# Shorter last chunks, weighted two fours per round, in the attention layers of a graph network kernel

## The reference

```
xj = gl[src]                                       # gathered by edge
e = leaky_relu(xj + gr[dst] + edge_e, 0.2)
alpha = einsum('ehc,hc->eh', e, att_w)             # 4 heads of 32 channels
m = segment_max(alpha, dst); alpha = exp(alpha - m[dst])
denom = segment_sum(alpha, dst); alpha = alpha / (denom[dst] + 1e-16)
out = segment_sum(xj * alpha[..., None], dst) + bias
```

## Time and profile before

| | us |
|---|---|
| median of 3 runs | 8513.38 |
| lowest, highest | 8485.4, 8525.23 |
| the profiled execution, its own time | 8425.69 |
| its span | 8423.3 |
| attention layers, first copy of the first to L2080 of the last | 4345.1 to 8380.8 |

### The profile page before, as it was taken

The page is one execution under the profiler, slowest core; times in us unless marked ns, Lnnn a source line. Parts: engine busy times, 40 slices in busy tenths (PEclk is TensorE's granted clock), DMA queues, the critical chain, the costliest instruction groups (busy, mean ns, idle before and its releaser), DMA issues.

```text
span 8423.3 us, 124315 instructions
## 1 busy us (share of the span) xinstructions
PE 5549.1 (66%) x35700; PEld 4942.3 (59%) x35700; DVE 3931.2 (47%) x13695; ACT 3368.8 (40%) x12586; POOL 4633.3 (55%) x4868
## 2 busy tenths in 40 slices
PE   7445555577777667777746766765666675767676
PEld 5333333566667566677646666664666664666665
DVE  4222222366666566665644444452444443444445
ACT  2222221366666456666623333332333332333333
POOL 2555554366666356666426666626666653666562
PEclk9999999899998888888868888887888886888887
DMA  2110010344444234444313333323333332333332
GB/s 56 22 25 24 23 24 19 100 106 103 106 104 106 65 104 121 124 120 118 94 52 108 107 108 109 108 79 93 108 107 108 107 106 67 109 107 107 106 108 64
DMA packets 489685, 743.91 MB, mean 88 GB/s; under 512 B 219285, under 2 KB 351865, under 8 KB 487973
## 3 DMA queue, kind: packets, MB, share of 16 engines
q1 hardware_dynamic: 307764, 423.98, 16.2%
q0 software_dynamic: 180928, 305.59, 15.1%
q10 hardware_dynamic: 320, 6.40, 0.3%
HBM read 636.97 MB, written 97.83 MB: 87 GB/s over the span
## 4 chain that ended last, share of the span: by engine, by line
PE 18%; issue 13%; another core or an unknown queue 13%; DVE 12%; ACT 5%; DVEq 3%; POOL 0%; ACTq 0%; DMA 0%
DVE AR L1956 5%; PE PS L1368 4%; PE PS L1382 3%; PE PS L1259 2%; PE PS L1283 2%; PE PS L1280 2%; PE PS L1380 2%; DVEq L505 1%; ACT AR L1040 1%; DVE AR L1877 1%; PE PS L1393 1%; DVEq L1956 1%; ACT AR L936 1%; ACT AR L1029 1%
## 5 line engine op out<-in xcount | busy, mean ns | idle before, releaser
L577 POOL DMA_INDIRECT AR<-gtab_d,AR x2436 | 2308.9, 948 | 1523.0 <-issue 625.1
L569 POOL DMA_INDIRECT AR<-ptab_d,AR x1624 | 1545.9, 952 | 1006.0 <-issue 397.3
L1040 ACT ACTIVATE AR<-PS,AR 128x512 f32<-128x512 f32 x609 | 418.5, 687 | 2511.7 <-PE PS L1382 1218.6
L1368 PE MATMUL PS<-AR 128*112 128x132 f32 x4872 | 927.9, 331 | 688.9 <-DVE AR L1956 665.3
L1956 DVE TENSOR_TENSOR AR<-AR,PS 112x132 f32 x2436 | 696.0, 286 | 1191.8 <-issue 448.9
L1368 PEld LDWEIGHTS PS<-AR 128*112 128x112 f32 x4872 | 727.5, 209 | 827.0 <-DVE AR L1956 420.4
L551 POOL DMA_INDIRECT rec_d<-AR x782 | 753.0, 963 | 654.8 <-DVE AR L1563 431.0
L1382 PE MATMUL PS<-AR 128*128 128x128 f32 x4872 | 1024.7, 312 | 27.3 <-issue 27.1
L2033 DVE SCALAR_TENSOR_TENSOR AR<-PS,AR 128x512 f32<-128x512 f32 x609 | 455.2, 747 | 998.3 <-issue 567.8
L1382 PEld LDWEIGHTS PS<-AR 128*128 128x128 f32 x4872 | 898.7, 230 | 29.1 <-issue 28.7
L1259 PE MATMUL PS<-AR 128*112 128x161 f32 x3248 | 673.4, 335 | 340.5 <-DVE AR L1877 175.9
(11 more groups left out here) (345 smaller groups left out, 8872.9 us busy)
## 6 DMA issues: line engine op xcount, KB each, us to landing
AR<-ste_d SPq DMA_DIRECT2D x404, 512.0 KB
AR<-nbb_d SPq DMA_DIRECT2D x303, 224.0 KB
ste_d<-AR SPq DMA_DIRECT2D x101, 512.0 KB
AR<-gtab_d,AR POOLq DMA_INDIRECT x2436
AR<-ptab_d,AR POOLq DMA_INDIRECT x1624
nbb_d<-AR SPq DMA_DIRECT2D x101, 224.0 KB
AR<-key_d SPq DMA_DIRECT2D x94, 224.0 KB
AR<-rec_d SPq DMA_DIRECT2D x812, 8.0 KB
```

The costliest lines, as they stand in the source:

```text
L569: e.indirect_dma_start(out=XJ1[:, t % 32, :], out_offset=None, in_=tabs_d[0][:, :], in_offset=off).then_inc(done_, 16)
L577: e.indirect_dma_start(out=xj2(t)[:, t % 4, :], out_offset=None, in_=tabs_d[1][:, :], in_offset=off).then_inc(done_, 16)
L1368: x = e.matmul(PS[6 + v_ % 2][0:B, (t % 2) * 132:(t % 2 + 1) * 132], SQ4[:, i % 4, t % 4, :], PX[:, i % 5, t % 4, :, :].rearrange("p c h - ...
```

## The change

The ends of the chunks were 8, 16, ..., 184, 190, 195, 199, 203. They are now 8, 16, ..., 176, 182, 187, 192, 196, 200, 203: the last six chunks have 6, 5, 5, 4, 4 and 3 fours instead of the last five having 8, 6, 5, 4 and 4. There are 28 chunks instead of 27. Fours of chunks that end after 176 are weighted two per round, so that a chunk's fours are no longer spaced one per round behind its `back`. DVE gets the second weight of a round behind `leaked` and one add; ACT spreads the second four of a round behind the copy. `LASTR` falls from 217 to 211.

```diff
 def rounds_of_attention():
-    ends = list(range(8, 185, 8)) + [190, 195, 199, NQ]
+    ends = list(range(8, 177, 8)) + [182, 187, 192, 196, 200, NQ]
...
         back = max(turn + 3, px[-1] + 1 if px else 0)
         steps.append((turn, turn + 1, turn + 2, turn + 2, back))
-        px += [back + i for i in range(end - start)]
+        per = 1 if end <= 176 else 2
+        px += [back + i // per for i in range(end - start)]
...
+            def spread_out(l, i):
+                w.wait_ge(*nl_sem(l, i))
+                if i >= 4:
+                    w.wait_ge(s_scat2, pair_at(l, 2 * (i - 4) + 1))
+                done(e.activation(SQ4[:, i % 4, :, :], NBB[:, nb_slot(l, i), :, :], ACT.Copy), s_oh2)
...
-                    for i in weighted_in(j):
-                        w.wait_ge(*nl_sem(l, i))
...
+                    spread = weighted_in(j)
+                    for i in spread[:1]:
+                        spread_out(l, i)
                     if 0 <= j < NQ:
...
                         done(e.activation(LE[:, j % 2, :], PS[j % 2][:, :], ACT.Identity, bias=BRS[:, l % 2:l % 2 + 1], scale=0.2), s_le)
+                    for i in spread[1:]:
+                        spread_out(l, i)
...
                     if j < NQ:
                         leaked(j)
+                    if len(quads) > 1:
+                        add()
+                        weight(quads[1])
                     while tiles:
                         add()
```

More of the change, by code:

```diff
@@ L31, in rounds_of_attention @@
 def rounds_of_attention():
-    ends = list(range(8, 185, 8)) + [190, 195, 199, NQ]
+    ends = list(range(8, 177, 8)) + [182, 187, 192, 196, 200, NQ]
     px, steps, start = [], [], 0
-    for c, end in enumerate(ends):
+    for end in ends:
         turn = end + 1
@@ L1030, in scalar_program @@
                         done(x, s_ex)
-                    for i in weighted_in(j):
-                        w.wait_ge(*nl_sem(l, i))
-                        if i >= 4:
-                            w.wait_ge(s_scat2, pair_at(l, 2 * (i - 4) + 1))
-                        done(e.activation(SQ4[:, i % 4, :, :], NBB[:, nb_slot(l, i), :, :], ACT.Copy), s_oh2)
+                    spread = weighted_in(j)
+                    for i in spread[:1]:
+                        spread_out(l, i)
                     if 0 <= j < NQ:
```

## The result

The changed kernel has a median of 8531.27 us (22 runs, 8509.59 to 8750.88); the kernel before, run beside it, 8508.38 us (22 runs). The ratio is 1.0024, 95% interval 1.0016 to 1.0032: slower by 0.24%, some 20 us. The forecast was 19 us faster. The measured median lies inside the stated range of 8456 to 8536, near its slow end, but on the other side of the kernel before. One execution of the changed kernel (8750.88, granted clock 0.644) was in a slower state and is not in the ratio.

What follows compares the result with a forecast made beforehand. Gathers were taken to gate rounds at about 5.9 us, with PE and DVE limiting the tail. Per layer -16.1 + 0.5 + 4.1 + 5.1 = -6.4, three layers -19 us: median 8513 to 8494, range 8456 to 8536.

Steps and rivals of the forecast that it cites:

- The tail: From copy 202 to a layer's end: seven fours left to weight instead of twelve, 47.6 becomes 31.5 us, a gain of 16.1.
- rival 4: The tail shrinks only to 40 us, as two chunks back to back; +2.1 per layer, 8520 us; chance 0.08.
- Rounds 196 to 202: Stretch before the tail: nine fours as before but bunched, two fresh returns; 30.9 against 30.4 us, a loss of 0.5.
- The late load: One-hots of fours 186 and 187, loaded too late for round 193: copy 193 starts 5.1 us late, once per layer.
- Rounds 188 to 195: Stretch beside the gathers with five more fours: 53.6 against 49.4 us, a loss of 4.1 per layer.
- gate of 5.9: Pace of about 5.9 us per round while POOL gathers, leaving PE and DVE some 2 us to spare.
- two-four chain: Copy, relu, add, weight, add before the fourth scat at 2.6 us; a round with two fours costs 7.2 by itself.
- rival 3: Rounds 188 to 202 run at half clock because of new PE gaps; +7.6 per layer, 8536 us; chance 0.05.
- Rival 2: Two-four rounds 190 to 194 each pay 3.4 us on top of the gate; +6.5 per layer, 8533 us; chance 0.15.
- break-even: Rival 2's limit: below 2.6 us extra per round the layer is still not slower.
- What costs nothing: 28th chunk's masks, small DVE instructions and DMAs, and the spread moved behind the copy: 0, at most 4 us in all.
- The last sign: The prediction is wrong if the layers outside these stretches change by more than a few us.

Runs made afterwards that it cites:

- run 1: Changed kernel with the one-hots of fours 186 and 187 loaded one step of SP's list earlier; ratio 0.999 to the kernel before.
- run 14: Changed kernel with the early load, without the gathers of fours 188 to 202 and PE's waits for them, slow-gather chip; ratio 0.9902 to the kernel before.
- run 3: Changed kernel with six of eight adds, instead of two, ahead of the leaky relu in rounds that scatter two fours; ratio 0.9974 to the kernel before.
- run 15: Changed kernel with early load, third and fourth scat behind the second half, four adds ahead of the leaky relu, slow-gather chip; ratio 0.996 to the kernel before.
- run 2: Changed kernel's 28 chunks with one four weighted per round, as before the change; ratio 1.0 to the kernel before.
- run 6: Changed kernel with early load, third and fourth scat behind the second half, four adds ahead of the leaky relu, fast-gather chip; ratio 0.994 to the kernel before.
- run 11: The three edits of run 6 to the changed kernel again, on another fast-gather chip; ratio 0.9945 to the kernel before.
- run 5: Changed kernel with the third scat of a two-four round behind the second half, next to the fourth, fast-gather chip; ratio 0.999 to the kernel before.
- run 10: The kernel before again, unedited, for its profile on a fast-gather chip; ratio 1.0002 to the kernel before (6801.54 us).
- run 16: Kernel before with the attention layers' gathers of a round issued in two pairs, slow-gather chip; ratio 1.0028 to the kernel before.

## Why the prediction was wrong

The way was wrong: 19 us faster were forecast, some 20 us slower were measured. The mechanism that it named for the gain is there, and so are the places of the losses. In the third layer the losses were sized 13 us too small together, and the gain 3 us too large.

- **The tail**: forecast -16.1, measured -12.8 to -13.8 (34.0, 33.8 and 34.4). Inside the stated range; rival 4 (40 us) is out. (The terms of the forecast add up to 31.1, not 31.5.)
- **Rounds 196 to 202**: forecast +0.5, measured +1.8 to +2.1. Inside the range.
- **The late load**: forecast 5.1. Copy 193 stands 5.3 us behind its data, so the step was right, but taking the load earlier gives back 8.0 to 9.2 (run 1). What was missed is the cost behind the wait: PE runs at half clock into round 194 (2.3 us of it in that round).
- **Rounds 188 to 195**: this is the step that failed, "such a round costs 7.2 by itself ... Against a gate of 5.9 only the excess counts". Without the late load the stretch is 62.5 instead of the forecast 53.6 (run 1). Two errors of 6 us each, with 3 us too much in rounds 188, 189, 191 and 195 against them. First, in round 190 the hold and the two-four chain do follow each other (12.3 instead of 6.5; 7.3 without gathers, run 14). Second, rounds 192 to 194 are 9 to 10, 9 and 8 us long without any gather (7.2, 7.2 and 6.4 forecast): in 192 and 193 PE's granted clock falls behind the wait for the adds (0.81 to 0.83 and 0.64 to 0.81 granted, run 14), and in 194, at 1.00, the third scat makes the second half wait 1.06 us for two adds. What DVE does to the fourth scat was counted rightly (2.53 measured, 2.6 forecast), the clock and the third scat's wait were not; the clock was rival 3, priced for rounds 196 to 202 and with a chance of 0.05.
- **Rival 2**, the one slower than before, came closest in size: its 8533 is within 2 us of the measured median. That is partly luck, since it is right for round 190 only and has neither the clock nor the full price of the late load (+6.5 per layer forecast; 9 to 11 in the profiles from copy 171 on). Its break-even is also wrong: with 10.5 us to spare per layer and five rounds it is 2.1 us per round, not 2.6. Its place, the fourth scat behind the second half, is confirmed by run 3 for rounds 192 to 194; in round 190 it is the third scat (run 15 with run 3: moving adds alone left it at 12.3, moving the third scat as well gave 7.9, with 2 to 4 us of that coming back in round 191).
- **What costs nothing**: right. The additional chunk and the short chunks by themselves make no difference (run 2).
- **The last sign**, that the layers must not change outside these stretches, reads wrong by the profiles: up to copy 171 they differ by 17.8, 14.1 and 0.0 us. Runs 1 to 3, with the same 28 chunks, took 1082 to 1096 us there, before 1080 to 1095, so this is how much executions and chips differ and not the change.

In the sum: -13.2 + 1.9 + 21 instead of -16.1 + 0.5 + 9.2 in the third layer. That the loss is the order and the late load and not the idea is shown by runs 6, 11 and 15: the same chunks and the same rounds of weighting, with three edits, are 0.4 to 0.6% faster than the kernel before on three chips. How much of it each of the three edits carries is known only in part: the load (run 1) and the adds (run 3) by themselves, the third scat by itself only on a fast-gather chip (run 5).

## What to carry to other kernels

When work is doubled in a round of a pipeline written out by hand, the price is not the second piece's own time but what it puts between two engines: look for every place where the new instruction waits for an answer and stands ahead of the work that the next engine waits for, and try it behind that work. A list of loads that is tied to rounds must be moved with the rounds. And price a new wait of PE with the half clock that follows it, as the rows of another stretch show it.

## What the runs showed of the hardware

- The same kernel takes 8433 to 8508 us on some chips and 6793 to 6802 us on others, 20% less. Each gather takes POOL 1.25 us on both. On the fast-gather chips the gated round takes 5.0 us and POOL hardly waits (run 10); on the slow-gather chips 5.9, and engines that wait for PE start up to 4.7 us after it is done, some 3 us after the start of the last of a series of gathers (round 190 above); without gathers they start 0.1 us after it (run 14). Leaving out the last 60 gathers of a layer took the ratio from 0.999 (run 1) to 0.9902 (run 14) on slow-gather chips. What differs between the chips no run here shows.
- Issued in two pairs, the gathers hold PE no shorter (run 16).
- Inside an otherwise busy round, a wait of PE of 2.58 us stood ahead of some 5.7 us of work at the lower clock, 1.2 GHz (0.64 granted over a round of 9.6 us), without any gather beside it (run 14). The granted clock had fallen within the wait. One of 1.76 us in the next round of that run left it at 1.00. In run 15, where the scats waited 0.2 to 0.6 us, the stretch from copy 191 to copy 193 was granted 1.00:

```profile
8256.37:8262.64 6.27, 4.92 (x38) 4.18 (x37) 3.88 (x11) 2.54 (x7) 3.83 (x5) 1.00 0.71 218
8262.64:8268.81 6.17, 5.34 (x40) 4.51 (x39) 5.12 (x16) 2.53 (x8) 3.89 (x5) 1.00 0.21 47
```
